# A three-stage Perceiver kernel on one core: unread products in TensorE's waits, two products cut into pieces, one product moved ahead of a transpose

## What is computed

```
x = x + L0_xattn(ctx, layernorm(x))     # 16 heads of 64; keys from 256 context rows and 64 latents
x = x + L0_attn(layernorm(x))           # linear attention: q, k = relu(...); kv = k^T v; out = q kv / (q sum k)
x = x + L0_ffn(layernorm(x))            # silu(x Wg^T) * (x Wu^T), then Wd^T; hidden size 768
x = x + L1_xattn(layernorm(x), ctx)     # 16 heads of 16, masked softmax over 256 context rows
x = x + L1_attn(layernorm(x))           # a gated cell scanned over the 64 tokens
x = x + L1_ffn(layernorm(x))            # 8 experts relu(x W1 + b1) W2 + b2, weighted by an entmax router
```

## Time and profile before

| what | us |
|---|---|
| runs of the kernel before: lowest, median, highest | 2092.19, 2093.69, 2097.15 |
| the profiled execution: its time, its span | 2092.97, 2091.2 |
| TensorE busy in the span | 2030.2 (97%) |
| VectorE, ScalarE, GpSimd busy | 1206.1, 1123.8, 498.0 |
| mean granted TensorE clock, share of full | 0.992 |

### The profile page before, as it was taken

How to read it: one execution, slowest core, us unless ns; L and a number is a source line. 1 busy time by engine, 2 the same in 40 slices (tenths; PEclk the granted TensorE clock), 3 DMA queues, 4 the chain that set the end, 5 groups by cost and what they waited for, 6 DMA issues and landing times. The chain is left out here.

```text
span 2091.2 us, 46297 instructions
## 1 busy us (share of the span) xinstructions
PE 2030.2 (97%) x18801; PEld 1822.3 (87%) x18801; DVE 1206.1 (58%) x3626; ACT 1123.8 (54%) x2556; POOL 498.0 (24%) x411
## 2 busy tenths in 40 slices
PE   7999999999999999699899999999999999999998
PEld 6999999999999999377778888788999999999998
DVE  6756565556565655567668899735938723233311
ACT  5556555656565655333258787644444444444443
POOL 1000020000000000123311222144444444444444
PEclk9999999999999999899999999999999999999999
DMA  4000200000000000100031110100110101101000
GB/s 151 22 17 22 77 22 17 22 16 22 17 22 17 23 16 2 46 1 1 1 87 43 33 32 22 42 1 7 55 41 1 41 1 41 41 1 41 1 11 31
DMA packets 48786, 57.81 MB, mean 28 GB/s; under 512 B 6528, under 2 KB 40128, under 8 KB 48448
## 3 DMA queue, kind: packets, MB, share of 16 engines
q1 hardware_dynamic: 48576, 54.85, 8.1%
HBM read 46.72 MB, written 2.10 MB: 23 GB/s over the span
## 5 line engine op out<-in xcount | busy, mean ns | idle before, releaser
L935 POOL TENSOR_TENSOR right_h<-right_hr,right_h 128x512 fp32r<-128x512 f32 x256 | 341.0, 1332 | 420.8 <-ACT right_hr L1256 420.8
L1255 ACT ACTIVATE right_h<-bank,dec_b 128x512 fp32r<-128x512 f32 x256 | 176.2, 688 | 392.7 <-PE bank L83 371.3
L83 PE MATMUL bank<-lat_wv,lat_kv_t 128*128 128x256 f32 (+1 forms) x1728 | 258.9, 300 | 0.7 <-issue 0.7
L83 PE MATMUL bank<-lat_kv_t,lat_qk 128*128 128x320 f32 x1536 | 254.7, 315 | 0.0
L83 PEld LDWEIGHTS bank<-lat_kv_t,lat_qk 128*128 128x128 f32 x1536 | 226.3, 188 | 7.7
L2218 ACT ACTIVATE lat_p<-bank,lat_neg_max 128x320 f32<-128x320 f32 x256 | 136.3, 532 | 173.7 <-DVE lat_neg_max L2342 173.7
L83 PEld LDWEIGHTS bank<-lat_wv,lat_kv_t 128*128 128x128 f32 x1728 | 223.0, 190 | 6.8 <-issue 1.1
L83 PE MATMUL bank<-dec_xt,dec_lo 128*128 128x512 f32 x512 | 200.7, 392 | 0.0
L1256 ACT ACTIVATE right_hr<-bank,dec_b 128x512 f32<-128x512 f32 x256 | 174.5, 682 | 0.0
L1737 POOL TENSOR_TENSOR lat_rs_rstdc<-lat_rs_varc,lat_rs_halfc 128x4 f32<-128x4 f32 x16 | 16.2, 1015 | 635.4 <-DVE lat_rs_varc L1729 635.4
L1104 PE MATMUL bank<-dec_hi,right_h 128*128 128x256 f32 x1024 | 161.6, 279 | 1.2 <-POOL right_h L935 1.2
(11 more groups left out here) (325 smaller groups left out, 3912.2 us busy)
## 6 DMA issues: line engine op xcount, KB each, us to landing
raw_w<-in_L_ffn_W SPq DMA_DIRECT2D x16, 1024.0 KB, 6.5
lat_ctx_raw<-in_ctx SPq DMA_DIRECT2D x16, 512.0 KB, 4.2
right_ctx_raw<-in_ctx_turned SPq DMA_DIRECT2D x16, 512.0 KB, 3.7
lat_kv_t<-lat_lt SPq DMA_DIRECT2D x32, 128.0 KB, 2.1
out_x<-x_sb SPq DMA_DIRECT2D x4, 512.0 KB, 2.9
x_sb<-in_x SPq DMA_DIRECT2D x1, 1792.0 KB, 14.7
lat_xl_now<-lat_xl SPq DMA_DIRECT2D x7, 256.0 KB, 4.8
ahead_room<-in_L_xattn_Wq SPq DMA_DIRECT2D x1, 1024.0 KB, 7.0
```

What stands on the lines that cost most here:

```text
L83: mm = pe.matmul(out, lhs(a, k), rhs(b, k), start=first and k == 0 and n == 0, stop=last and k == KD - 1 and n == 2)
L935: pool.tensor_tensor(h[:, g % 2, 1, :], hr[:, g % 2, :], h[:, g % 2, 0, :].bitcast(F32), ALU.subtract).then_inc(h_lo, 1)
L1255: act.activation(h[:, n % 2, 0, :], h_bank[n % 2][:, :], ACT.Relu, bias=bias).then_inc(h_hi, 1)
```

## The change

Five edits, on TensorE's order and in one place on ScalarE's.

1. `keep_awake(n)` issues `n` float32 products of `ident` with `wkv` (512 columns) into `gate_bank`, which nobody reads in the first chunk. They stand at six places of the first chunk: three ahead of `turn_rows(0)`, one ahead of `queries(0)`, one ahead of the fourth `contexts`, five ahead of `turn_ffn(0)`, two behind it.
2. `down_two` takes the place of `down` for tiles 0 and 1 of a chunk: the blocks 0 to 4 of tile 0, each as soon as `h_lo` counts it, then those of tile 1, then block 5 of both. The two counts of `down_psum` come at its end.
3. The last `project_output` of the first stage is cut into four pieces of six products, put around the two parts of the last `turn` and before and behind the last `weigh`.
4. `hidden(0, 0)` goes ahead of `turn(31, 1)`, with a wait for `s_low` because it writes a bank that held scores.
5. ScalarE reads the side step of b = 31 before its two exponentials (`cell_exps`), not behind them.

```diff
@@ -399,27 +399,51 @@
                     product3(pe, bank[:, :], lambda a, kd: wgu[:, a, kd, g, h * P:(h + 1) * P],
                              lambda a, kd: ft[:, a, kd, :]).then_inc(done, 1)
 
+            def down_piece(c, i, h):
+                for j, (a, b) in enumerate(PASSES):
+                    mm = pe.matmul(down_bank[i % 2][:, 0:D], ht[:, a, h, i * P:(i + 1) * P], wd[:, b, h, :],
+                                   start=h == 0 and j == 0, stop=h == NH - 1 and j == 2)
+                return mm
+
+            def down_two(c):
+
+                if c == 0:
+                    pe.wait_ge(wd_lo, 1)
+                for i in range(2):
+                    if c >= 1:
+                        pe.wait_ge(x_done, c * PER + i - 1)
+                    for h in range(NH - 1):
+                        if i == 0:
+                            pe.wait_ge(h_lo, NH * c + h + 1)
+                        down_piece(c, i, h)
+                pe.wait_ge(h_lo, NH * (c + 1))
+                for i in range(2):
+                    down_piece(c, i, NH - 1).then_inc(down_psum, 1)
+
             def down(c, i):
                 n = c * PER + i
-                if n == 0:
-                    pe.wait_ge(wd_lo, 1)
-                if n >= 2:
-                    pe.wait_ge(x_done, n - 1)
-                if i == 0:
-                    pe.wait_ge(h_lo, NH * (c + 1))
+                pe.wait_ge(x_done, n - 1)
                 for h in range(NH):
-                    for j, (a, b) in enumerate(PASSES):
-                        mm = pe.matmul(down_bank[n % 2][:, 0:D], ht[:, a, h, i * P:(i + 1) * P], wd[:, b, h, :],
-                                       start=h == 0 and j == 0, stop=h == NH - 1 and j == 2)
+                    mm = down_piece(c, i, h)
                 mm.then_inc(down_psum, 1)
 
+            def keep_awake(n):
+
+
+                for _ in range(n):
+                    pe.matmul(gate_bank[:, :], k.ident[:, :], wkv[:, 0, :], start=True, stop=True)
+
+            keep_awake(3)
             turn_rows(0)
+            keep_awake(1)
             queries(0)
             keys_values(0)
             for c in range(NCH):
                 for i in range(PER + 1):
                     if c >= 1:
                         gate_up(c - 1, i)
+                    elif i == PER:
+                        keep_awake(1)
                     if i >= 1:
                         contexts(PER * c + i - 1)
                     if i < PER:
@@ -433,18 +457,22 @@
                 if c + 1 < NCH:
                     queries(c + 1)
                 if c >= 1:
-                    down(c - 1, 0)
-                    down(c - 1, 1)
+                    down_two(c - 1)
                 if c + 1 < NCH:
                     keys_values(PER * (c + 1))
                 if c >= 1:
                     down(c - 1, 2)
+                else:
+                    keep_awake(5)
                 turn_ffn(c)
+                if c == 0:
+                    keep_awake(2)
                 if c >= 1:
                     down(c - 1, 3)
             for h in range(NH):
                 gate_up(NCH - 1, h)
-            for i in range(PER):
+            down_two(NCH - 1)
+            for i in range(2, PER):
                 down(NCH - 1, i)
 
         @block.scalar
@@ -1159,8 +1187,9 @@
                     side_step(*in_slot[b])
                 if b >= 2 and b % 2 == 0:
                     project_output(b // 2 - 1)
+            pe.wait_ge(s_low, 8 * B)
+            hidden(0, 0)
             turn(B - 1, 1)
-            hidden(0, 0)
             weigh(B - 1, 0)
             weigh(B - 1, 1)
             for n in range(1, E * STEPS):
@@ -1289,13 +1318,15 @@
                 turn(b, 0)
                 for r in range(R):
                     weights_of(b, 1, r)
+                if b == B - 1:
+                    side_read(*in_slot[b])
                 if b % 8 == 7 and b >= 15:
                     cell_exps(b // 8 - 1)
                 if b % 8 == 0 and b >= 16:
                     cell_tanh(b // 8 - 2)
                 if b in (17, 18):
                     expert0_high(b - 17)
-                if b in in_slot:
+                if b in in_slot and b < B - 1:
                     side_read(*in_slot[b])
             turn(B - 1, 1)
             for n in range(E * STEPS):
@@ -2072,17 +2103,18 @@
                 product3(pe, dst[:, :], lambda x, kd: kv_t[:, off % 2, x, kd, S2:S2 + P],
                          lambda x, kd: wv[:, x, kd, a * 512:(a + 1) * 512]).then_inc(l_psum, 1)
 
-            def project_output(c, off, _a):
+            def project_output(c, off, _a, of=range(NU)):
                 i = 2 * c + off
                 dst = free_bank(pe, "w", c, off, 0)
                 if i == 0:
                     pe.wait_ge(w_lo[3], 4)
-                pe.wait_ge(o_lo, NU // 2 * (i + 1))
-                for hp in range(NU):
+                pe.wait_ge(o_lo, NU // 2 * i + of[-1] // 2 + 1)
+                for hp in of:
                     for j, (x, y) in enumerate(PASSES):
                         mm = pe.matmul(dst[:, 0:D], at[:, x, hp, :], wo[:, y, hp, :], start=hp == 0 and j == 0,
                                        stop=hp == NU - 1 and j == 2)
-                mm.then_inc(w_psum, 1)
+                if NU - 1 in of:
+                    mm.then_inc(w_psum, 1)
 
             def energies(c, off, hp):
                 i = 2 * c + off
@@ -2094,9 +2126,10 @@
                     product3(pe, s_bank[b][:, 0:LK], lambda x, kd: qk[:, (NU * i + hp) % RING, x, kd, b, :],
                              lambda x, kd: kv_t[:, off % 2, x, kd, b * LK:(b + 1) * LK]).then_inc(s_psum, 1)
 
-            def turn(c, off, hp):
+            def turn(c, off, hp, parts=(0, 1)):
                 i = 2 * c + off
-                for n, tiles in enumerate(((0, 1), (2, 3, 4))):
+                for n in parts:
+                    tiles = ((0, 1), (2, 3, 4))[n]
                     pe.wait_ge(p_ready, 16 * i + 2 * hp + n + 1)
                     wait(pe, pt_done, 16 * i + 2 * hp - 1 + n)
                     for slot, t in enumerate(tiles):
@@ -2155,9 +2188,13 @@
                 do[kind](0, pair, a)
             for c in range(COUPLES):
                 couple(c, first=c == 0, last=c == COUPLES - 1)
-            turn(COUPLES - 1, 1, NU - 1)
+            project_output(COUPLES - 1, 1, 0, of=(0, 1))
+            turn(COUPLES - 1, 1, NU - 1, parts=(0,))
+            project_output(COUPLES - 1, 1, 0, of=(2, 3))
+            turn(COUPLES - 1, 1, NU - 1, parts=(1,))
+            project_output(COUPLES - 1, 1, 0, of=(4, 5))
             weigh(COUPLES - 1, 1, NU // 2 - 1)
-            project_output(COUPLES - 1, 1, 0)
+            project_output(COUPLES - 1, 1, 0, of=(6, 7))
 
         @block.scalar
         def _(act):
```

## The result

The changed kernel takes **2079.7 us** (median of 4 runs, 2078.6 to 2080.9), the kernel before 2092.9 us (median of 4 runs beside them, 2092.1 to 2097.2). The ratio is 0.993, 95% interval 0.9917 to 0.9943: 13.2 us less, where the prediction's terms made 12.0 and its time was 2081.3. The profiled execution took 2080.24 us, 12.73 less than that of before.

The account below looks back on a forecast made before the run. TensorE was taken as the bound, busy 2030.2 of 2091.2 us. Terms 1.9 + 0.8 + 3.7 + 0.1 - 1.1 + 3.55 + 3.05 = 12.0 us less gave a forecast of 2081.3 us, range 2078.8 to 2086.4.

Parts of the forecast that it names:

- Nothing behind is late: Step at the end of attention: `weigh`, normalisation, projection and the first expert's `output` move earlier together, keeping the 3.05 us.
- the end of the body: Term for `down` in pieces ahead of the decoder: the 2.92 us wait goes and 72 products run quicker, 3.55 us gained.
- First stage: Term for the stage's end: 18 products move up, saving 2.3 us, less 0.4 us of pushed `weigh`, 1.9 us gained.
- Seam: Term between first stage and body: unread products ahead of `turn_rows(0)`, clock taken to fall, 0.8 us gained, ends -0.8 and 2.3.
- The rival with a high clock: Rival where the body begins: the clock stays high, 1.5 us more gained, time 2079.5 us, chance 0.2.
- First chunk: Term for the body's start: unread products keep the clock high through `turn_ffn(0)` and `gate_up(0, 0)`, 3.7 us gained.
- Third and last chunk: Terms for `down` in pieces: 0.1 us gained in the third chunk, 1.1 us lost in the last.
- the wait moves from ahead of `down` to behind two tiles: Step in the last chunk: the third `down` waits 3.3 us for VectorE's `residual` of tile 0, so nothing is gained.
- The price of the low clock on the path: Last chunk: after the moved wait, 18 products, `turn_ffn(3)` and the next `down` run slow; 1.1 us lost, ends 0.1 and -1.9.
- Attention to experts: Term for `hidden(0, 0)` ahead of the last `turn`'s second part: `hidden(0, 1)` starts at 1346.65 instead of 1349.72, 3.05 us gained.
- a quick `weigh`: Step at the end of attention: the last `weigh` runs at the high clock in 1.1 us, where it took 1.94.
- the largest group of waits of TensorE: Reading of the profile before: `down` waiting for GpSimd's low half, 7.8 us in three waits.

## Why the prediction came near, and which step of it failed

The time came out 1.6 us below the forecast, near the low end of the range. Most terms were right in their mechanism. The step that failed is the overlap assumed behind the last `turn`, "Nothing behind is late": the projection was late by 0.84 us, and the term gave 2.25 us instead of 3.05. A second term, the end of the body, was sized too low. One by one:

**First stage.** Right: 2.0 against 1.9, the same in every profile with the pieces. Two small errors cancel: the pieces pushed the last `weigh` by 0.16 us and not 0.4, and six products instead of 24 gave 2.16 us and not 2.3.

**Seam.** The size, 0.8 against 0.73, was right for this pair of profiles, by a wrong reason: I put the fall down to a pause behind `weigh` together with the barrier's, and with the first filled it fell all the same. The rival with a high clock isn't another case but another draw: three profiles of ten had it, with 2.4 us. The Trainium skill (TensorE: Matmul & The Clock Gate, section "Why this matters for your kernels") warns only of longer gaps; here the clock was lost in seven of ten behind one of 1.85 us, and the measurement decides.

**First chunk.** Right in mechanism and size (3.99 against 3.7). Without the products the loss is there (3.3), with them alone the gain (3.96).

**Third and last chunk.** The step "the wait moves from ahead of `down` to behind two tiles" was right, down to its releaser, and so was the bound behind it (`fn`). The price of the low clock on the path was sized at 1.1 and measured 0.72, within its ends, but that is one draw: in eight profiles of kernels with this order from the third chunk on, the last chunk took 0.6 to 1.8 us more than in the profile of before, seven of them 0.6 to 0.8.

**End of the body.** The term was mis-sized, 3.55 against 4.12, outside its ends. I priced a product at 0.131 us, near the short rows (2.39 us for 18); in a long row at the high clock it is 0.124 (4.47 us for 36), which is 0.5 us on 72. More important, I took the low clock behind the old wait for a fixed cost. It was 1.4 us in one profile and nothing in two others.

**Attention to experts.** The step that failed is "Nothing behind is late: `weigh`, normalisation, projection and the first expert's `output` move together". `hidden(0, 1)` did start 3.14 us earlier (3.05 predicted). But VectorE's multiplication now began while GpSimd's subtraction ran and took 1.18 instead of 0.29 us, and 0.89 us went back. That GpSimd's instruction did it is shown: held back, it left the multiplication at 0.29 us and the stretch 0.88 us shorter. That the new order brought the two together is not: with the old order they met as well, once `weigh` ran at the high clock, and a quick `weigh` was a term of the prediction itself. I had read every engine's queue and not what two engines do to each other.

**A reading.** I called `down`'s 7.8 us the largest group of waits of TensorE. There was a larger one in the kernel before, 8.1 us in a single wait near the start of the program. The change doesn't touch it, and it is 8.1 us after, too.

**The sum** came out near partly by luck: -0.8 at the experts and +0.6 at the end of the body nearly cancel.

## What to carry to other kernels

Fill a wait with work only after asking what the next instruction waits for: the last chunk gained nothing from 30 products in a wait, because `fn` bound it, and lost the clock at a worse place. Where a kernel has pauses of about 2 to 4 us, as this one, a single profile is one draw of where the low clock falls; compare stretches of several profiles before a term is called measured. When work is moved earlier, look at what runs beside it on VectorE and GpSimd, not only at what it waits for.

## What the runs showed of the hardware

**VectorE is held up beside GpSimd.** The multiplication of 128x128 from two tensors in SBUF takes 0.29 us alone; begun while GpSimd's subtraction of 128x512 ran, it took 1.18 or 1.00 us and ended both times 0.15 us behind it. The trace shows this as a longer busy time of the multiplication, not as a wait. The Trainium skill states it (SBUF — State Buffer, section "Who interferes with whom"): a VectorE instruction with two inputs in SBUF contends with a GpSimd instruction that reads SBUF, the ports that they share are an exclusive lock, and the order of issue decides which of the two is blocked. The trace agrees, 1.18 against 0.29 us for the multiplication that began 0.26 us behind the subtraction.

**The clock's fall varies from execution to execution.** Behind a wait of 4.5 us it was low for some 3 us (before) or 7 (with `down` whole again). Behind the barrier's pause of 1.85 us it fell in seven profiles of ten. At the seam into the body it was low for up to 10 us (12.2, 11.6 and 13.0 us from the stage's end to the first `keys_values` without unread products). Behind the wait of 2.92 us at the end of the body it fell in one of three profiles. The times of the kernel before go with it: every execution of 2096.7 us and more had a mean granted clock of 0.988, every one below 2094.8 had 0.991 or 0.992.
